# The fourth pair of bracketing sums moved ahead of the router's products in a fused layer kernel

## The reference, cut to what matters

```python
h = tok(x)                                # embedding, softmax(q k) v
h = h + mixer(layernorm(h))               # in_proj, conv, SSD, gate, out_proj
h = h + ffn(layernorm(h))                 # router, top 2 of 8, experts

# in the mixer (SSD), for chunk c and head h:
Lm = exp(segsum(a))                       # 128x128 per head and chunk
Y_diag = einsum('bcln,bcsn,bhcls,bcshp->bclhp', C, B, Lm, X * dt)

# in the ffn:
scores = softmax(xf @ w_router)           # xf: 256 features, 8 experts
expert_weights, top_experts = top_k(scores, 2)
```

## Time and profile before

| what | value |
|---|---|
| median of 3 runs | 905.13 us |
| the profiled execution | 905.44 us |
| its span in the trace | 903.7 us |
| TensorE busy | 886.7 us (98%) |
| VectorE busy | 631.9 us (70%) |
| ScalarE busy | 530.4 us (59%) |
| GpSimd busy | 507.2 us (56%) |
| granted TensorE clock | full in all 40 slices |

### The profile page before, as it was taken

How to read it: one execution, slowest core, us unless ns; L and a number is a source line. 1 busy time by engine, 2 the same in 40 slices (tenths; PEclk the granted TensorE clock), 3 DMA queues, 4 the chain that set the end, 5 groups by cost and what they waited for, 6 DMA issues and landing times.

```text
span 903.7 us, 17534 instructions
## 1 busy us (share of the span) xinstructions
PE 886.7 (98%) x5705; PEld 785.4 (87%) x5705; DVE 631.9 (70%) x1708; ACT 530.4 (59%) x1106; POOL 507.2 (56%) x491
## 2 busy tenths in 40 slices
PE   8999999999999999999999998999999999999998
PEld 7888898888888888888888887899999999999997
DVE  2587889889888988898898864636464646464633
ACT  1677777677777777777777755344444444444433
POOL 5657877877888788778766352232233232323343
PEclk9999999999999999999999999999999999999999
DMA  7940111010001000000000116434343434332221
GB/s 214 325 163 13 36 48 32 20 42 23 24 12 26 13 23 13 26 14 20 17 4 13 48 31 215 118 72 117 71 113 74 110 75 103 79 85 53 24 59 47
DMA packets 49381, 59.11 MB, mean 65 GB/s; under 512 B 6288, under 2 KB 44667, under 8 KB 49344
## 3 DMA queue, kind: packets, MB, share of 16 engines
q1 hardware_dynamic: 35904, 42.14, 14.4%
q0 software_dynamic: 13440, 16.50, 10.7%
HBM read 33.62 MB, written 30.67 MB: 71 GB/s over the span
## 4 chain that ended last, share of the span: by engine, by line
PE 82%; DVE 4%; DMA 4%; SPq 3%; issue 3%; ACT 2%; POOL 1%; another core or an unknown queue 0%; DVEq 0%; POOLq 0%; ACTq 0%
PE bank L1666 12%; PE bank L1665 12%; PE bank L1667 12%; PE bank L1727 10%; PE bank L1870 5%; PE bank L1656 5%; PE bank L1838 4%; PE bank L1796 3%; PE bank L1711 3%; SPq L448 3%; DMA w_raw<-w 3%; PE bank L1693 2%; PE bank L1702 2%; PE bank L1686 2%; PE bank L2055 1%
## 5 line engine op out<-in xcount | busy, mean ns | idle before, releaser
L726 POOL DMA_INDIRECT out<-ye,tok_slot x56 | 95.7, 1710 | 229.8 <-DMA out<-ye,tok_slot 125.8
L920 ACT ACTIVATE hf<-bank 128x512 f32<-128x512 f32 x128 | 79.4, 620 | 184.0 <-PE bank L1667 181.4
L1114 DVE TENSOR_TENSOR h_lo<-hf,h_hi 128x512 fp32r<-128x512 f32 x128 | 88.6, 693 | 100.9 <-ACT h_hi L921 98.5
L1232 DVE SCALAR_TENSOR_TENSOR xc<-bank,cw,xc 128x253 f32<-128x253 f32 (+2 forms) x288 | 128.3, 470 | 1.7 <-ACT xc L836 0.2
L1665 PE MATMUL bank<-xe_hi,w_hi 128*128 128x512 f32 x256 | 101.0, 394 | 1.5 <-ACT h_hi L921 1.2
L1666 PE MATMUL bank<-xe_lo,w_hi 128*128 128x512 f32 x256 | 100.5, 393 | 0.0
L1667 PE MATMUL bank<-xe_hi,w_lo 128*128 128x512 f32 x256 | 100.4, 392 | 0.0
L663 POOL DMA_INDIRECT slots_dram<-rows,slot x64 | 64.6, 1010 | 52.6 <-DVE slot L1393 26.3
L921 ACT ACTIVATE h_hi<-bank 128x512 fp32r<-128x512 f32 x128 | 79.6, 622 | 0.0
L1665 PE MATMUL bank<-first_w_hi,h_hi 128*128 128x256 f32 x256 | 72.8, 284 | 2.5 <-DVE h_lo L1114 2.5
L1665 PE MATMUL bank<-w_hi,h_hi 128*128 128x256 f32 x256 | 73.0, 285 | 0.0
(11 more groups left out here) (266 smaller groups left out, 2624.1 us busy)
## 6 DMA issues: line engine op xcount, KB each, us to landing
w_raw<-w SPq DMA_DIRECT2D x16, 1024.0 KB
slots_dram<-zero_row SPq DMA_DIRECT2D x1, 8320.0 KB, 29.7
xe<-slots_dram SPq DMA_DIRECT2D x16, 520.0 KB, 4.6
out<-hb SPq DMA_DIRECT2D x16, 256.0 KB, 2.1
w_raw<-in_wT SPq DMA_DIRECT2D x2, 644.0 KB, 5.9
out<-zero_row SPq DMA_DIRECT2D x1, 1024.0 KB, 32.0
slots_dram<-rows,slot POOLq DMA_INDIRECT x64
out<-ye,tok_slot POOLq DMA_INDIRECT x64
```

The lines of the kernel that those rows point to most:

```text
L726: g.indirect_dma_start(out, bass.IndirectOffsetOnAxis(ap=tok_slot[q][:, j:j + 1], axis=0), ye[q][:, j, :], None, compute_op=ALU.add).then_ ...
L920: sc.activation(hf[m % 2][:, :], h_bank[i % H_BANKS][:, :], ACT.Gelu_apprx_tanh).then_inc(hf_ready, 1)
L1114: vc.tensor_tensor(h_lo[:, m, :], hf[m % 2][:, :], h_hi[:, m, :].bitcast(F32), ALU.subtract)\
L1232: ins = vc.scalar_tensor_tensor(out=xc[p][:, m, back:], in0=bank[p][XBC_BANK[i]][:, h * L:(h + 1) * L - back], scalar=cw[:, m, TAPS - 1 - ...
```

## The change

In TensorE's list, `segment_sums(b, q, 3)` moves from behind `route(t, p)` to right behind `segment_sums(b, q, 2)`. In halves that have both `b` and `t`, the two products of the fourth pair now run ahead of the router's products. In halves without `t` the order is as it was. No other engine's list changes, and no instruction is added or removed.

```diff
                 if b:
                     x_to_rows(b, q, 1)
                     segment_sums(b, q, 2)
+                    segment_sums(b, q, 3)
                 if t:
                     route(t, p)
                 if b:
-                    segment_sums(b, q, 3)
                     chunk_state(b, q)
                     own_chunk(b, q, 0)
                 if not b:
```

## The result

The kernel with the change takes 907.87 us (median of 15 runs, 906.82 to 908.32), the kernel before 905.23 us in the same comparison (median of 15). The ratio is 1.0028, with a 95% interval of 1.002 to 1.0035: 2.6 us slower. Its profiled execution took 907.88 us, 2.44 us over that of before, with a span of 906.1 us.

The account below looks back on a forecast made before the run. The bound was taken as a chain crossing TensorE and VectorE (`attend`, router's products, L1348, VectorE's list to L1161). 11 regular halves times 0.32 us, plus 0, plus 0.4, less 0.2, gave 3.7 us: 908.8 us, range 904.6 to 912.9.

Parts of the forecast that it names:

- the narrow range: Whole kernel: the forecast's own case, a time of 907.8 to 910.6 us, chance 0.50.
- Steps 1 and 2: TensorE, VectorE: fourth pair costs 0.56 us ahead of the router's products (0.86 us); L1348 and `xdt` come 0.56 us later.
- Step 3: TensorE at `own_chunk(b, q, 0)` (L1838): it waits for the later `xdt` and stands for 0.38 us.
- Step 5: GpSimd and VectorE: L599 takes 0.19 us, L620 gets ahead of L1274, which ends at 299.16; L1367 is not held up.
- step 2: VectorE: L1348 starts at 296.11 in place of 295.55, 0.56 us later, and `xdt` follows with the same offset.
- Step 6: VectorE: `y` of chunk 0 comes 2.80 us after L1274's end, 0.32 us later; 0.24 of 0.56 us are taken up.
- Step 7: TensorE at `to_yT`: its 0.38 us are covered by 0.41 us of standing; VectorE makes the half 0.32 us longer.
- The other three halves: First half costs 0, the last 0.4 us into the drain, the next to last gains 0.2 us, at most 0.47.
- the whole delay stays: Rival: L1274 gets ahead of the first L620, everything behind is 0.56 us later in 14 halves, 912.9 us; chance 0.22.
- faster: Rival: the router's first weights no longer wait for `v2T` (2.8 us in all), VectorE's delay is covered, 901.9 us; chance 0.06.

Follow-up runs that it names:

- the run of both edits: The changed kernel with ScalarE's exponential of the fourth pair ahead of the router's and VectorE's `xdt` ahead of L1348: 904.49 us, ratio 0.9994 to the kernel before.
- all chunk work first: The changed kernel with the fourth pair's exponential ahead of the router's on ScalarE, and `xdt` and L1274 ahead of L1348 on VectorE: 905.63 us, ratio 1.0006.
- half of the delay: Against the kernel before, only `seg_hi` of the fourth pair moved ahead of the router's products, `seg_lo` left behind them: 905.10 us, ratio 1.0006.
- the last pair of experiments: GpSimd's L599 moved behind the two L620, in the kernel before (904.34 us, ratio 0.9994) and in the changed kernel (905.93 us, ratio 1.0013).

## Why the prediction was right

The sign and the way the loss comes about were forecast, and 907.87 us lies in the narrow range (907.8 to 910.6), but by 0.07 us alone. 3.7 us of loss were forecast and 2.6 measured. By its steps:

- Steps 1 and 2 had the mechanism right and the size too large. The term "costs 0.56 us" for the fourth pair was read where the pair stands behind the router's products. Right behind another pair it costs 0.46 us, as TensorE's rows show: its first product costs 0.23 us there and 0.32 us behind the others. The router's products cost 0.81 us in place of 0.86. L1348 came 0.42 us later, not 0.56.
- Step 3: TensorE's L1838 came 0.32 us later, where 0.38 were forecast. The two are that near because two errors go against each other: the router's smaller delay alone would have made it 0.24 us (0.42 less 0.24, plus 0.06), but L1838 starts 0.15 us behind the end of `xdt` (298.30 to 298.45) and not 0.06. By `to_hT` TensorE is 0.41 us late (7.17 and 7.58), because the L1838 behind the stand take 0.08 us more. In a regular half this was covered, as forecast: with `xdt` first the stand is gone and the halves stay at 31.1 us.
- Step 5: L1274's end at 7.82 us behind `attend` is what was forecast (299.16 less 291.34), because it hangs on L620's start (5.70, as forecast) and no longer on the router. That is why the error of step 2 did no harm to the sum, and it was luck: the forecast had L620 first by 0.28 us (297.04 and 297.32), and it was first by 0.07. In the next to last half L1274 did get ahead (5.78, L620 at 5.88), and L1367 took 0.95 us there.
- Step 6: `y` came 0.24 us later in place of 0.32. The 2.80 us from L1274's end to `y` were read from the last half; a regular half has 2.72 us. This term is most of the difference between 3.5 and 2.3 us for the regular halves. The rest is the first regular half, which grew by 0.10 us only, since VectorE was ahead there, and 0.02 us or so in the others.
- Step 7 and the signs: that TensorE would no longer stand at L1796 and `attend`, and that its cover would be "nearly used up", was wrong, and does not follow from the prediction's own sums. A half that VectorE makes 0.32 us longer gives TensorE 0.32 us of new cover, so 0.35 of the 0.41 us would have been left. In the half shown TensorE still stands for 0.10 us at L1796 (291.63 to 291.97, less 0.24) and 0.16 us at `attend` (292.68, less 291.97 and 0.55), 0.26 us in all. The views of waits (60 to 500 us), before and then after:

```profile
PEld bank L1711 <- DVE v L1161: 6.0, 14, 0.4
PEld bank L1796 <- issue: 5.4, 12, 0.5
...
PEld bank L1711 <- DVE v L1161: 5.9, 14, 0.4
PEld bank L1796 <- issue: 3.4, 11, 0.3
```

- Two more signs came out larger than forecast, for the reasons of steps 1 to 3: L1838 starts 1.33 us after L1823 in place of 1.24, and L1274 takes 2.05 us in place of 1.8, since it is issued earlier and ends when forecast.
- The other three halves: 0, 0.4 and a gain of 0.2 were forecast. The first cost 0.12 us and not 0. `y` comes at 10.13 as before, so VectorE is not later, as forecast, but TensorE comes to `to_yT` 0.40 us later (10.33 and 10.73), and its cover is smaller in that half: 0.27 us (30.74 less 10.33 and less the 20.14 us of the rule below). In the next to last, L597 takes 0.20 us, and TensorE no longer waits for `hn`, as forecast; the distance behind it went from 31.24 to 30.96 us, a gain of 0.28. From the last `attend` to the end of the span it is 0.30 us more (426.72 and 427.02). With the regular halves that is 0.12 plus 2.31 less 0.28 plus 0.30, the 2.4 us between the two spans.
- The rival "the whole delay stays" (the first of the list, which the prediction once calls the second) was decided as written, by who is first. The run in which GpSimd may not get in first is this rival, made: `y` is 0.41 us later, 0.06 us of it by the wait itself. At the smaller size of step 2 its price is 0.35 us a half, not 0.56.
- Of the rival "faster" one half came: the wait of the router's first weights for `v2T` is gone from the changed kernel's view of waits. No gain came with it.

One step is better told by the runs than by the prediction. "TensorE's 0.38 us are covered by the 0.41 us" is one case of a rule with two terms: the half is the longer of `y` plus 20.59 us and `to_yT` plus 20.14 us, both counted from `attend`. The first constant is before's 30.89 less 10.30, the second is that of the run of both edits, 30.94 less 10.80. They give 31.13 (10.54 plus 20.59) for the changed kernel, where 31.12 was measured, 31.14 (10.55) for `xdt` first, where it was 31.11, 31.30 (10.71) for the run in which GpSimd may not get in first, where it was 31.24, and by the second term 30.82 (10.68) for all chunk work first and 30.88 (10.74) for L599 late in the changed kernel, both as measured. The first half of the changed kernel is of the second kind too: 30.87 (10.73), and 30.86 measured. With half of the delay the first term is 0.03 to 0.14 us too long (31.01 for 10.42 and 30.93 measured, 30.89 for 10.30 and 30.75 to 30.86 measured). The constants are read from these runs and may not hold elsewhere.

No version clearly beats the kernel before. With the exponential of the fourth pair first, alone or with `xdt`, the move costs 1.0 us or nothing that can be told (905.81 and 904.49 us against 904.86); that it is of use is not shown. What stays open is where the shorter halves of the last pair of experiments go in the median, and whether a place for L597, L599 and L620 exists that lets L1274 start at 5.0 us without `hn` coming late.

## What to carry to other kernels

In hand-ordered lists, moving work ahead of a short operation that others wait for is paid by everything behind that wait on the other engines, even if the engine that moves has no more to do; look first whether the reader of the moved result stands behind the same wait. The price is read from offsets to one recurring event, for each engine that can set the period (here VectorE's `y` and TensorE's `to_yT`), and not from busy time: GpSimd's fell by 9.3 us while the kernel became slower. Where instructions of VectorE and GpSimd exclude each other, as L1274 and L1367 do here with L599 and L620, one that runs five times its usual time is a wait: list who is issued first and by how much, since a shift of some tenths of a microsecond turns the order round, and the price of a delay then jumps or vanishes.

## What was not expected of the hardware

- A product of 128x512 right behind others with the same operand `below_r` costs 0.23 us; as the first behind products of another kind it costs 0.31 to 0.32 us. A pair is 0.46 or 0.55 us by its place.
- L599, an instruction on 128x2 elements, takes 0.19 us alone and 1.16 to 1.27 us when issued while L1274 runs. With half of the delay the two are issued within 12 ns of each other in eleven halves, and L599 takes 0.19 us in six of them and 1.26 to 1.27 us in five.
- Two L620 that stand right behind each other do not keep VectorE out: L1274, issued 0.07 us behind the first, gets in between them, and the two take 3.03 us in place of 2.04.
- Half of the delay cost 0.5 us (within the uncertainty), all of it 2.6 us: the relation between a delay and its cost was not proportional.
